# Attention on one core: the value products of each key block made singly, two key blocks behind their scores, in place of two in a row at every second key block

## What is computed

```
scores = jnp.einsum('bhqd,bhkd->bhqk', q, k) / jnp.sqrt(jnp.asarray(hd, x.dtype))
scores = jnp.where(causal, scores, jnp.asarray(-jnp.inf, x.dtype))
attn = jax.nn.softmax(scores, axis=-1)
y = jnp.einsum('bhqk,bhkd->bhqd', attn, v)
...
x = x + _layernorm(_L0_attn_ref(_layernorm(x, axis=-1), ...), axis=-1)
x = x + _layernorm(_L0_ffn_ref(_layernorm(x, axis=-1), ...), axis=-1)
```

## Time and profile before

| | us |
|---|---|
| median of 3 runs | 1303.68 (1301.52 to 1308.1) |
| profiled execution, its own time | 1300.54 |
| its span in the trace | 1298.6 |
| PE busy in the span | 1142.8 (88%) |
| DVE busy | 721.0 (56%) |
| ACT busy | 507.5 (39%) |

### The profile page before, as it was taken

How to read it: one execution, slowest core, us unless ns; L and a number is a source line. 1 busy time by engine, 2 the same in 40 slices (tenths; PEclk the granted TensorE clock), 3 DMA queues, 4 the chain that set the end, 5 groups by cost and what they waited for, 6 DMA issues and landing times. The chain is left out here.

```text
span 1298.6 us, 18975 instructions
## 1 busy us (share of the span) xinstructions
PE 1142.8 (88%) x7036; PEld 773.0 (60%) x7036; DVE 721.0 (56%) x968; ACT 507.5 (39%) x1058; POOL 269.3 (21%) x261
## 2 busy tenths in 40 slices
PE   3999998389999999999999994883999999999996
PEld 1777887145445444444444433662787787887785
DVE  4756755376777777777777513894223423324323
ACT  3133223025666666666666652441111111111111
POOL 1524524701111111111111111663000100001001
PEclk9999999558999999999999966886999999999998
DMA  7346346862444443434430005882100200200200
GB/s 259 97 112 171 112 115 180 160 105 50 77 84 89 85 77 76 75 75 75 76 75 19 18 25 177 254 284 81 65 1 1 97 1 2 98 1 17 81 1 33
DMA packets 82515, 113.01 MB, mean 87 GB/s; under 512 B 24964, under 2 KB 42500, under 8 KB 82436
## 3 DMA queue, kind: packets, MB, share of 16 engines
q1 hardware_dynamic: 82436, 111.92, 34.2%
HBM read 68.83 MB, written 42.21 MB: 86 GB/s over the span
## 5 line engine op out<-in xcount | busy, mean ns | idle before, releaser
L700 ACT ACTIVATE prob<-ps_s 128x512 f32<-128x512 f32 (+3 forms) x768 | 314.9, 505 | 190.1 <-PE ps_s L811 181.5
L723 DVE TENSOR_REDUCE neg<-ps_m 128x2 f32<-128x1024 f32 (+2 forms) x224 | 248.8, 1147 | 108.7 <-PE ps_m L781 73.8
L811 PE MATMUL ps_s<-q_op,k_op 50*128 50x512 f32 (+2 forms) x768 | 264.2, 449 | 29.0 <-ACT prob L700 26.0
L776 PE MATMUL ps_m<-k_op,q_op 48*128 48x512 f32 (+2 forms) x768 | 200.9, 428 | 34.4 <-DMA vg<-v_groups 23.0
L811 PEld LDWEIGHTS ps_s<-q_op,k_op 50*128 50x128 f32 x768 | 122.7, 192 | 158.7 <-ACT prob L700 93.8
L678 POOL TENSOR_SCALAR_AFFINE_SELECT prob<-prob 128x512 f32<-128x512 f32 x128 | 81.6, 637 | 445.1 <-ACT prob L700 445.1
L825 PE MATMUL ps_y<-prob,vg 128*17 128x512 f32 (+3 forms) x1536 | 155.6, 525 | 0.6 <-POOL prob L678 0.6
L1216 DVE TENSOR_TENSOR hf<-sl,ps_u 128x512 f32<-128x512 f32 (+1 forms) x44 | 30.2, 687 | 189.4 <-PE ps_u L72 189.4
L776 PEld LDWEIGHTS ps_m<-k_op,q_op 48*128 48x128 f32 x768 | 103.4, 199 | 51.4 <-issue 23.7
L723 DVE TENSOR_REDUCE neg_far<-ps_m 128x4 f32<-128x512 f32 (+2 forms) x96 | 97.6, 1045 | 37.9 <-PE ps_m L781 37.9
L1285 PE MATMUL ps_d<-w_ffn_high,wp_high 128*128 128x512 f32 (+1 forms) x352 | 115.6, 391 | 0.0
(11 more groups left out here) (161 smaller groups left out, 1769.2 us busy)
## 6 DMA issues: line engine op xcount, KB each, us to landing
raw<-in_w_ffn SPq DMA_DIRECT2D x16, 520.0 KB, 5.5
k_op<-k_parts SPq DMA_DIRECT2D x32, 256.0 KB, 5.1
q_op<-q_parts SPq DMA_DIRECT2D x64, 128.0 KB, 6.0
y_heads<-y_sb SPq DMA_DIRECT2D x32, 256.0 KB, 5.0
v_groups<-v_out SPq DMA_DIRECT2D x16, 272.0 KB, 3.9
vg<-v_groups SPq DMA_DIRECT2D x16, 272.0 KB, 6.9
x<-in_x SPq DMA_DIRECT2D x4, 1024.0 KB, 12.8
q_parts<-part_h SPq DMA_DIRECT2D x16, 256.0 KB, 2.9
```

Source lines behind the costliest of these rows:

```text
L700: act.activation(prob[:, v % NPROB, h, unit_cols(u)], ps_s[:, y % NS, unit_cols(u)], ACT.Exp, scale=D ** -0.5).then_inc(s_exp, 1)
L723: nc.vector.tensor_reduce(to[:, :, pairs[0]:pairs[-1] + 1, i - TT * c], scores, axis=AX.X, op=ALU.max, negate=True).then_inc(a_read, 1)
L776: last = nc.tensor.matmul(ps_m[:, g % 2, s, base:base + wide], q_op[buf][r, c, pair, (i - TT * c) * P:(i - TT * c + 1) * P], k_op[buf][r, ...
L811: nc.tensor.matmul(ps_s[:, y % NS, lo:BLK], k_op[buf][r, pair, j * P:(j + 1) * P], q_op[buf][r, c, pair, lo:BLK], start=True, stop=True)\
```

## The change

PE makes one `product` after every u, that of u - 2, where it made two (u - 2 and u - 1) after every even u. The two copies out of `ps_y` move one u later in ACT's order, since the products that they wait for do.

```diff
@@ scalar engine
-                    if u == 0 and n:
+                    if u == 1 and n:
                         take_y(n - 1, 1)
-                    if u == TT:
+                    if u == TT + 1:
                         take_y(n, 0)
             take_y(NG - 1, 1)
@@ tensor engine
                         score(n, u, pair)
                         for g in beside[n, u, pair]:
                             for_maxima(g)
-                    if u % 2:
-                        continue
-                    for back in (2, 1):
-                        if u:
-                            product(n, u - back)
-                        elif n:
-                            product(n - 1, NU - back)
+                    if u >= 2:
+                        product(n, u - 2)
+                    elif n:
+                        product(n - 1, NU + u - 2)
             for back in (2, 1):
                 product(NG - 1, NU - back)
```

## The result

The changed kernel takes 1371.34 us (median of 4 runs, 1368.62 to 1374.12) against 1305.89 us before (1301.52 to 1327.12 over 4 runs). The ratio of the fast runs, which leaves out the 1327.12, is 1.056 on record, with an interval of 1.0505 to 1.0614; the two medians alone give 1.050. 1314 us, 1297 to 1338, had been forecast. The profiled execution took 1370.81 us.

A forecast was written before the change was run, and what follows sets the result against it. The prediction took a ring of PE and ACT waiting for each other in turn to bound the attention. 1300.5 us profiled + 7 (ring) + 4 (clock) = 1311.5, with the median 3.1 above that 1314 us, range 1297 to 1338.

The forecast's parts named there:

- The likeliest case: Whole kernel: a moderate loss as summed, 1314 us, by itself 1307 to 1324; chance 0.45.
- the ring: PE and ACT waiting for each other in the attention: 0.5 us more a group, +7 us over 15 groups.
- the clock: PE's clock in the attention: 15 to 20 us more at the low level, +4 us.
- the links M, P and R: Fourth score to products, products to next score, that score to next fourth: M+P+R replaces ACT's pace at odd u.
- odd mark to odd mark: Fourth score of one odd u to the next: six stretches, summing to 31.2 us a group against 30.7.
- M of u8: Fourth score to products at u8: 2.09 us before, 1.67 after, as DVE gets time to catch up.
- thin stretch: Between u11 and the product of u0: products of 256 and 128 columns alone, nearly as thin as where the clock fell.
- the upper bound: Clock term: a fall in many groups lasting until u6, ten times 15 us at 0.25 us each, +37.
- Rival 1: Attention ring closes faster: single products fill PE's waits for ACT, -8 us, about 1296 us; chance 0.13.
- rival 2: Attention: no change, M of the odd u is met by DVE's waits that go, 1304 with 6 either way; chance 0.27.
- Rival 3: PE alone bounds: every layout switch adds, nothing else moves, +18 us, 1322; counted within the moderate loss, 0.45.
- Rival 4: PE's clock in the attention: falls that no double batch ends, 1325 to 1345 us; chance 0.15 at full size.

The follow-up runs named there:

- h3: The changed kernel with every score of u10 made twice: 1396.66 us.
- e3: The changed kernel with the products of u0 and u1 together behind u2, all others single: 1327.94 us.
- h2: The kernel before with the fourth score of u7 in group 3 alone made seven times, as a delay: 1296.97 us.
- e5: The kernel before with every score of u8 in group 3 alone made three times, as a delay: 1298.84 us.
- f1: The changed kernel with every score of u1 and u2 made three times: 1319.83 us.
- e6: The kernel before with the maxima behind the second score pair of each even u set between its two products: 1326.73 us.
- g2: The mixed order of e8 with the second and third score of u0, u3, u4 and u11 made twice: 1291.52 us.
- e4: The changed kernel with single products one key block behind their scores in place of two: 1362.69 us.
- e1: The changed kernel with every score of u1 and u2 made twice: 1324.41 us.
- e8: Mixed order against the kernel before: singles at u1, u2, u6 and u7, doubles at u0, u4, u8 and u10: 1321.89 us.
- e2: The changed kernel with every score of u9 and u10 made twice: 1321.58 us.

## Why the prediction was wrong

The likeliest case had two terms, +7 us for the ring and +4 for the clock.

**The ring was right.** 31.26 us a group against 31.2 forecast; the links M, P and R came out within 0.1 us, and so did each stretch from odd mark to odd mark, so the sum owes nothing to errors that cancel. M of u8 was 1.69 against 1.67, so DVE's wait went as reckoned. The term is +0.54 x 15 = 8 us, with 7 forecast. ACT's waits became more frequent and shorter, as I wrote, though not near 0.5 us at every u: they lie between nothing and 1.80. PE's own waits for exponentials, which I expected to be more frequent, were fewer between 300 and 700 us, 61 in place of 78 (those of its weight loads 198 in place of 182).

**The step that failed is the estimate of the clock**: "15 to 20 us more at the low level, +4 us". Its mechanism was named, that the double batches after which the clock came back are gone and that a nearly thin stretch remains; its size was wrong by fifteen times. It was ten falls of 17.1 us, 61 us together. The sum had 15 to 20 us more at the low level; behind group 0 it was ten times 17.1. Two readings led there. First, I took twelve steady groups without a fall for a property of the order, though group 1, with the same instructions, had fallen. The changed order falls or doesn't with the timing (groups 2, 6 and 10 against the rest; 14 of 14 in h3), so a thin stretch that is passed 15 times has to be priced 15 times. I also ranked stretches by the time of their products, "no stretch is quite so thin", and that does not sort them: the clock stayed up over 0.00 us of products in steady groups of before, and fell behind 0.61 us here. What makes the changed order fall so much more often is left open between timing and the content of the stretch. What makes each fall dear, the missing double batch, is shown by e3 for the falls at u0 to u2. Second, the upper bound was ten falls of 15 us at 0.25 us each, +37. Each fall cost 6.1 us in 17.1, 0.36 us a us. I had the rate from group 0, by setting it against a steady group, and it was too low there too: in h2 and e5, whose group 0 has before's instructions, it took 32.93 us with 10.1 of them at the low level and 37.82 with 24.1, which is 0.35 us a us. Ten falls of 17.1 us at 0.36 is the measured number. So the bound had the count right, but nothing on record led to ten, and that is luck; I gave it a chance of 0.15.

Group 0 took 3.3 us longer, near the half of the clock term that was meant for it. But the same instructions of before took 32.93, 36.77 and 37.82 us there (h2, before, e5), so two single executions don't show that the change did it.

**The rivals.** Rival 1 (the waits vanish) is refuted by the undisturbed group, which is 0.54 us longer and not shorter, and rival 2 (they balance, within 6 us) narrowly, by its 8 us. Rival 3 (switches alone) is refuted as the cause of the 5%: f1 has all the switches of the changed kernel and more matmuls, and is 51 us faster; its price is real but small, e6's 0.7 us a group. Its 18 us took 0.19 us for the way into and out of a batch together, where the words beside it, 0.13 and as much again, make 0.26 and 25 us; e6 measured 0.12. The Trainium skill, TensorEngine Tiling (Array Packing), Key Properties, has the rule weighed there, that a change of the tiling mode drains the engine; e6's 0.7 us a group agrees with a price, and it explains at most that. Rival 4 is what happened, beyond its stated 1345.

## What to carry to other kernels

Where two engines wait for each other in turn, add up the links from mark to mark; it gave the new length of a group to 0.1 us, and an order with products behind two odd key blocks whose group is 0.47 us shorter. But see also what each reordering does to the thinnest few microseconds of PE's work and to what follows them: with a double batch behind it a fall of the clock cost 1.5 us here, with single products 3.5 to 9.8. One group of a loop that fell while its equals did not is a warning: look at the clock of every round, not at its mean. PE's waits can be filled with repeated matmuls; in g2 that cost 0.02 us a group.

## What the runs showed that I had not expected

The clock fell while PE was busy by the trace for 3.02 of 3.40 us (e3, and e4 likewise), and it stayed up (0.97) in e3 where PE was busy for 4.95 of 5.70, a smaller share. So the busy share does not tell the two apart, and no run here shows what does. A kernel with useless matmuls was faster than the same without them, by 46 us with 128 of them in e1, and by 30 us with as many in g2 against e8. And two edits that differ only in whether u9 is repeated beside u10 took 1321.58 us (e2) and 1396.66 us (h3), with one fall against fourteen; the 64 scores between them change both the work and the timing, and which of the two counts these runs don't separate.
